# Feed-forward input of a ViT tower: normalising on ScalarE and weighing on GpSimd in place of VectorE

## Chip, cores and metric

One NeuronCore of a Trainium2 chip runs the whole program. The metric is device microseconds of that core for one execution. Before the change it is 2668.47 us (median of 3 runs, 2664.71 to 2668.48).

## The reference, cut to what matters

Four images become 12544 tokens of width 192, which go through a token attention, a linear attention, a routed feed-forward layer, a second attention and a quantised feed-forward layer. The change lies in the last of these:

```python
def rmsnorm(x, g):
    return x * jax.lax.rsqrt(jnp.mean(x * x, axis=-1, keepdims=True) + EPS_NORM) * g
def activation_quant(x):
    scale = 127.0 / jnp.maximum(jnp.max(jnp.abs(x), axis=-1, keepdims=True), EPS_Q)
    return jnp.clip(jnp.round(x * scale), -128, 127) / scale
...
h = bitlinear(x, w_in, g_in)
up, gate = jnp.split(h, 2, axis=-1)
y = jax.nn.silu(gate) * up
return bitlinear(y, w_out, g_out)
...
h = h + _L1_ffn_ref(_layernorm(h, axis=-1), L1_ffn_w_in, L1_ffn_g_in, L1_ffn_w_out, L1_ffn_g_out)
```

The layer norm and the RMS norm behind it come down to one factor per token: the input of the first product is (h - mean) * fac * g_in, which is then scaled by its largest absolute value and rounded to whole numbers.

## The kernel before

The last phase, `attention_and_ffn_phase`, handles the second attention and then the feed-forward layer. Tokens stand in `h` as 112 partitions by 112 tiles of 192 values. Four tiles are a group (448 tokens), and there are 28 groups (`NC`), seven to an image. The attention loop runs over s = 0 to 27; the feed-forward loop over g = 0 to 27 follows, and its first part (group 0 and the first input) is woven into the end of the attention loop. In the groups g = 1 to 7 (called the late groups here) the attention's output of the last image is added too (`map_late` on TensorE, `add_half` on VectorE); from g = 8 on there is only the feed-forward work.

There is no scheduler: each engine has a block of code, issues its instructions in the order written there, and waits at semaphores that are written out by hand. An instruction that waits holds up all that stands behind it on its engine.

One group g goes round as follows.

- VectorE, `quant_in(g+1)` (L2479 on): from the largest absolute value of each token to the scale `sx` and the output scale `dx`, with two small products by `fac` on the way (L2482, L2486), then four rounding instructions (L2488) and one that writes the whole numbers (L2493).
- VectorE, `weigh_in(g+2)` (L2464): four instructions write (h - mean) * gin to the single buffer `xg`; `largest_in(g+2)` (L2470) reduces it.
- TensorE, `into(g, q)` (L2048): two products per tile q = 0 to 3, the gate half and the up half. ScalarE, `silu(g, q)` (L2230); VectorE, `gated(g, q)` (L2501) multiplies the halves to `y`.
- GpSimd, `weigh(g, 0)` and `weigh(g, 1)` (L1872): y * gout for tiles 0, 1 and for tiles 2, 3, as `yg5`. VectorE, `largest_y(g, 0)` and `(g, 1)` (L2510) reduce these pairs. ScalarE, `squares(g, q)` (L2240) sums the squares; VectorE, `mean_square(g)` (L2506), and GpSimd, `root_of(g)` (L1877), make of them a factor per token.
- VectorE, `quant_y(g)` (L2525 to L2537): small instructions, the last of which (L2532) writes the scale `s2`, then the rounding of tiles 2 and 3. ScalarE, `scaled_y(g)` (L2247) rounds tiles 0 and 1 and `whole_y` (L2253) writes the whole numbers.
- TensorE, `transpose_y(g)` (L2060), ScalarE `take_y(g)` (L2259), TensorE `outof(g, pair)` (L2081), VectorE `result(g, pair)` (L2547), and SyncE stores the group.

ScalarE's order in a group is `scaled_y(g-1)`, `whole_y`, `take_y(g-1)`, squares 0, silu 2, squares 1, silu 3, squares 2, squares 3, `take_x(g+1)`, silu 0 and 1 of group g+1. The instruction of VectorE's `weigh_in` and GpSimd's loop are these:

```python
ins_ = nc.vector.scalar_tensor_tensor(xg[:, q, :], h[:, t, :], mean[:, t:t + 1], gin[:], ALU.subtract, ALU.mult)
...
for g in range(NC):
    weigh(g, 0)
    weigh(g, 1)
    root_of(g)
```

`fac` is made by GpSimd in one instruction for the first 64 tiles (`factor5(0, ...)`, L1864) while the attention loop ends, and in two more behind groups 8 and 9 for the rest.

Of the kernel before, what the change touches and what calls it, by code (L numbers as in the profile page):

```python
# [10 lines left out]
ACT = mybir.ActivationFunctionType  # L11
ALU = mybir.AluOpType
# [5 lines left out]
D = 192  # L18
KC = 96
T = 112  # L20
# [1630 lines left out]
def attention_and_ffn_phase(nc, ins, h, bns, mean, rstd, var, minus, eye, rows_out, out):  # L1651
# [9 lines left out]
    with ExitStack() as ctx:  # L1661
# [64 lines left out]
        fac = sb("fac5", [T, NT])  # L1726
        dif = rstd
        xg = sb("xg5", [T, TPC, D])
        xr = rows[:, TPC * HID:TPC * HID + TPC * D].rearrange("p (q d) -> p q d", q=TPC)
# [27 lines left out]
        def pga(g, q):  # L1757
# [10 lines left out]
                  "sg_out", "y_out", "yg_out", "ssq_out", "r2_in", "r2_out", "yq_out", "ytr_mm", "yT_out", "o_mm",  # L1768
                  "o_out", "stored", "dvec", "dvec2", "xg_out", "am_out", "fac_in", "fac_out", "scaled", "d2_out",
                  "xr_out", "yr_out", "s2_out", "ya_out")  # L1770
# [35 lines left out]
        def _(pool):  # L1806
# [59 lines left out]
            def weigh(g, pair):  # L1866

                for q in (2 * pair, 2 * pair + 1):
# [3 lines left out]
                    nc.gpsimd.tensor_tensor(yg5[:, q, :], y[:, q, :], gout[:], ALU.mult).then_inc(F["yg_out"], 1)  # L1872

            def root_of(g):

                pool.wait_ge(F["r2_in"], g + 1)
                nc.gpsimd.tensor_tensor(r2[:], ms2[:], mhalf5[:, 0:TPC], ALU.pow).then_inc(F["r2_out"], 1)  # L1877

            factor5(0, slice(0, HEAD))
            pool.wait_ge(F["gin_in"], 32)  # L1880
            for g in range(NC):
                weigh(g, 0)
                weigh(g, 1)
                root_of(g)
                if g in (AFTER, AFTER + 1):
                    half = HEAD + (g - AFTER) * (NT - HEAD) // 2
                    factor5(1 + g - AFTER, slice(half, half + (NT - HEAD) // 2))
# [260 lines left out]
        def _(act):  # L2148
# [77 lines left out]
            def silu(g, q):  # L2226
                act.wait_ge(F["in_mm"], g * TPC + q + 1)
                if 1 <= g * TPC + q <= TPC:
                    act.wait_ge(F["y_out"], g * TPC + q)
                nc.scalar.activation(sg[q % 2 if g else 0], pga(g, q)[0:T], ACT.Silu, scale=dx[g % 2][:, q:q + 1]).then_inc(  # L2230
                    F["sg_out"], 1)

            def squares(g, q):

                if g * TPC + q:
                    act.wait_ge(F["ssq_out"], g * TPC + q)
                if q == 0 and g:
                    act.wait_ge(F["r2_in"], g)
                act.wait_ge(F["y_out"], g * TPC + q + 1)
                nc.scalar.activation(junk5, y[:, q, :], ACT.Square, accum_out=ssq[:, q:q + 1]).then_inc(  # L2240
                    F["ssq_out"], 1)
# [14 lines left out]
            def take_y(g):  # L2256
                for half in range(2):
                    act.wait_ge(F["ytr_mm"], 2 * g + half + 1)
                    nc.scalar.copy(yT[:, 2 * half:2 * half + 2, :],  # L2259
                                   pyt[:, half, 0:2 * CH].rearrange("p (k c) -> p k c", k=2)).then_inc(F["yT_out"], 1)  # L2260

            take_x(0)
            silu(0, 0)
            silu(0, 1)
            for g in range(NC):
# [7 lines left out]
                squares(g, 1)  # L2273
                silu(g, 3)
                squares(g, 2)
                squares(g, 3)
# [10 lines left out]
        def _(dve):  # L2287
# [171 lines left out]

            def weigh_in(g):  # L2460

                for q in range(TPC):
                    t = g * TPC + q
                    ins_ = nc.vector.scalar_tensor_tensor(xg[:, q, :], h[:, t, :], mean[:, t:t + 1], gin[:],  # L2464
                                                          ALU.subtract, ALU.mult)
                ins_.then_inc(F["xg_out"], 1)

# [11 lines left out]
            def quant_in(g):  # L2479
                dve.wait_ge(F["fac_out"], 1 if (g + 1) * TPC <= HEAD else 3)  # L2480
                dve.wait_ge(F["am_out"], g + 1)
                scaling(nc.vector.tensor_tensor(am[:], am[:], fac[:, g * TPC:(g + 1) * TPC], ALU.mult))  # L2482
                scaling(nc.vector.tensor_scalar(am[:], am[:], 1e-5, 1.0 / 127, ALU.max, ALU.mult))
                nc.vector.tensor_scalar(dx[g % 2][:], am[:], wsc[0:T, 0:1], None, ALU.mult)
                scaling(nc.vector.reciprocal(sx[:], am[:]))
                scaling(nc.vector.tensor_tensor(sx[:], sx[:], fac[:, g * TPC:(g + 1) * TPC], ALU.mult))  # L2486
                for q in range(TPC):
# [69 lines left out]
            for s in range(-3, NC):  # L2557
# [30 lines left out]
                if s == NC - 2:  # L2588
                    dve.wait_ge(F["gin_in"], 32)
                    weigh_in(0)  # L2590
                    largest_in(0)
                if s == NC - 1:
                    quant_in(0)
                    weigh_in(1)
                    largest_in(1)
            gram_turned(B - 1)
# [7 lines left out]
            map_projected(B - 1)  # L2604
            add_half(NC - LATE + 1, 1, 0)
            quant_in(1)
            gated(0, 2)
            largest_y(0, 0)
            image_mapped(B - 1)
            weigh_in(2)  # L2610
            gated(0, 3)
            largest_in(2)
            mean_square(0)
            largest_y(0, 1)
            quant_y(0)
            for g in range(1, NC):
                late = NC - CPI + g - 1
                if g + 1 < NC:
                    quant_in(g + 1)
                if g + 2 < NC:  # L2620
                    weigh_in(g + 2)
                gated(g, 0)
                gated(g, 1)
                if g + 2 < NC:
                    largest_in(g + 2)
                gated(g, 2)
# [10 lines left out]
                if late < NC:  # L2637
                    add_half(late, 1, 0)
                result(g - 1, 1)
                quant_y(g)  # L2640
                if g == AFTER:
                    finish(1, slice(HEAD, NT))
            result(NC - 1, 0)
            result(NC - 1, 1)
# [110 lines left out]
```

## Time and profile before

| | |
|---|---|
| median of 3 runs | 2668.47 us |
| the profiled execution's own time | 2666.92 us |
| its span | 2665.1 us |
| granted TensorE clock, mean of the span | 0.912 of full speed |
| TensorE matmul busy, whole span | 84% |
| VectorE busy | 72% |
| ScalarE busy | 60% |
| GpSimd busy | 39% |

The span is one execution, seen by the hardware profiler. Busy shares are averages over phases with different limits, so the last phase has to be read by itself: the feed-forward loop lies between some 2234 us and the end. The timeline lists instructions in order of time, merged where the same instruction repeats; in square brackets is the idle time of the engine just before, and who ended it.

### The profile page before, as it was taken

What the parts mean: (1) busy time and instruction counts of PE and PEld (TensorE: products, weight loads), DVE (VectorE), ACT (ScalarE), POOL (GpSimd) and SP (SyncE); (2) the same over time, 40 slices, a digit from 0 to 9 for tenths busy, and PEclk for the clock granted to TensorE, in tenths of its full rate; (3) what the DMA queues carried; (4) which work ended last, traced back from release to release, by engine and by line L of the source; (5) the groups of instructions that cost most, each with busy time, mean ns of one, the idle gap of its engine ahead of it and who ended that gap; (6) DMA issues with size and microseconds to landing.
All of it is one profiled execution on the core that took longest, in us unless ns stands there. A gap on an engine that the chain in (4) does not pass through costs nothing. (4 is left out here: it accounts for less than half of the span.)

```text
span 2665.1 us, 45416 instructions
## 1 busy us (share of the span) xinstructions
PE 2250.9 (84%) x14046; PEld 1626.4 (61%) x14047; DVE 1924.3 (72%) x5417; ACT 1594.4 (60%) x2815; POOL 1040.1 (39%) x1101
## 2 busy tenths in 40 slices
PE   8999999999997899999982999991778887766655
PEld 4444444444443788888871999991667775544443
DVE  5777777777774688888872566664558778889896
ACT  2444444444443688888861676663778764667776
POOL 1100100100000167667673577676555533353433
PEclk9999999999998899999985999996779998777777
DMA  2000000000000333233235677777756720000000
GB/s 59 0 19 13 0 18 13 1 9 1 0 0 23 87 66 75 67 73 76 66 71 165 219 242 240 246 242 133 94 71 87 91 30 6 22 22 26 22 27 26
DMA packets 114522, 183.08 MB, mean 69 GB/s; under 512 B 14337, under 2 KB 84326, under 8 KB 114078
## 3 DMA queue, kind: packets, MB, share of 16 engines
q0 software_dynamic: 74816, 86.34, 17.3%
q1 hardware_dynamic: 39554, 94.84, 11.1%
q8 instruction: 80, 1.31, 0.2%
q14 instruction: 72, 0.59, 0.1%
HBM read 64.44 MB, written 64.39 MB: 48 GB/s over the span
## 5 line engine op out<-in xcount | busy, mean ns | idle before, releaser
L213 ACT ACTIVATE prob<-pscore 128x896 f32<-128x896 f32 x336 | 308.1, 917 | 423.5 <-PE pscore L295 423.5
L420 DVE TENSOR_REDUCE pmax<-ppre 112x1 f32<-112x512 f32 x656 | 424.3, 686 | 162.0 <-PE ppre L262 161.9
L309 PE MATMUL pout<-prob,xkey 128*64 128x448 f32 x1344 | 328.0, 567 | 0.4 <-ACT prob L213 0.4
L1578 POOL DMA_INDIRECT rows_out<-yb,home3b x252 | 244.5, 970 | 141.8 <-issue 59.3
L262 PE MATMUL ppre<-xh,yh 49*112 49x512 f32 x656 | 291.3, 446 | 7.8 <-DVE pmax L420 4.1
L195 POOL CAST yh<-ynext 113x448 fp32r<-113x448 f32 x28 | 17.2, 616 | 667.3 <-DVE pmax L420 639.2
L737 POOL DMA_INDIRECT rows_in<-xr,idx x224 | 235.1, 1050 | 76.3 <-issue 44.8
L262 PEld LDWEIGHTS ppre<-xh,yh 49*112 49x112 f32 x656 | 112.6, 172 | 239.5 <-issue 103.5
L295 PE MATMUL pscore<-yh,xh 49*128 49x448 f32 x700 | 241.2, 422 | 0.4 <-DVE yh L440 0.4
L1872 POOL TENSOR_TENSOR sums<-rows,gout 112x512 f32<-112x512 f32 x112 | 141.2, 1270 | 253.2 <-DVE rows L2501 253.2
L295 PE MATMUL pscore<-yh,xl 49*128 49x448 f32 x700 | 202.9, 364 | 0.0
L295 PE MATMUL pscore<-yl,xh 49*128 49x448 f32 x700 | 142.8, 364 | 0.0
L2060 PE MATMUL ptr<-eyeb,wT 112*128 112x112 bf16 x448 | 45.3, 292 | 114.1 <-ACT wT L2253 114.1
L1485 PE MATMUL pz<-xth3b,wd 128*128 128x448 f32 x504 | 140.7, 381 | 0.0
L1500 PE MATMUL py<-uph,zl 128*112 x504 | 131.8, 261 | 0.0
L1500 PE MATMUL py<-upl,zh 128*112 x504 | 131.6, 261 | 0.0
L1500 PE MATMUL py<-uph,zh 128*112 x504 | 131.5, 261 | 0.0
L309 PEld LDWEIGHTS pout<-prob,xkey 128*64 128x64 f32 x1344 | 66.6, 135 | 105.7 <-issue 85.3
L295 PEld LDWEIGHTS pscore<-yh,xl 49*128 49x128 f32 x700 | 127.9, 187 | 0.8
L1935 PE MATMUL pqk<-xh,wh 128*128 128x448 f32 x168 | 72.1, 429 | 56.4 <-ACT spent L2196 55.8
L2060 PEld LDWEIGHTS ptr<-eyeb,wT 112*128 112x128 bf16 x448 | 38.9, 141 | 126.8 <-ACT wT L2253 88.9
L1472 PE MATMUL ptr3b<-eye,xb 112*128 112x112 f32 x504 | 63.5, 271 | 61.9 <-DMA xb<-rows_in 42.8
(393 smaller groups left out, 6647.2 us busy)
## 6 DMA issues: line engine op xcount, KB each, us to landing
wd<-down SPq DMA_DIRECT2D x63, 512.0 KB
xb<-rows_in SPq DMA_DIRECT2D x63, 455.0 KB
sums<-rows_out POOLq DMA_DIRECT2D x56, 336.0 KB, 6.1
h<-brow POOLq DMA_DIRECT2D x28, 336.0 KB, 5.2
h<-gambet POOLq DMA_DIRECT2D x28, 336.0 KB, 4.9
out<-sums SPq DMA_DIRECT2D x28, 336.0 KB, 2.8
rows_in<-zero SPq DMA_DIRECT2D x15, 455.0 KB, 5.5
rows_out<-yb,home3b POOLq DMA_INDIRECT x252
```

The source lines that it names most:

```text
L213: nc.scalar.activation(prob[j % 3][:, :, :], pscore[j % 2][:, :, 0:CH], ACT.Exp).then_inc(exped, 1)
L262: pe.matmul(out[:, :], yh1[rows, q * T:(q + 1) * T], xh[b % 2][rows, block * 512:(block + 1) * 512], start=True, stop=True, tile_position= ...
L295: mm = pe.matmul(pscore[j % 2][:, i, 0:CH], x[b % 2][rows, keys], y[rows], start=(n == 0), stop=(n == 2), tile_position=(i * LO, 0))
L309: mm = pe.matmul(pout[i * LO:(i + 1) * LO, 0:CH], xkey[b % 2][:, 2 * j + i, :], prob[j % 3][:, i, :], start=(j == 0), stop=(i == 1 and j = ...
L420: nc.vector.reduce_max(pmax[:, q, 2 * block + half:2 * block + half + 1], bank(u, depth), AX.X).then_inc(pre_max, 1)
L737: nc.gpsimd.indirect_dma_start(rows_in, bass.IndirectOffsetOnAxis(ap=idx[r % G3][:, 2 * q + k:2 * q + k + 1], axis=0), xr[r % G3][:, q, :] ...
L1485: mm = pe.matmul(pz[m][:, 0:CH], wd[i][:, w, cols], x, start=(s_ == 0), stop=(s_ == 4))
L1500: mm = pe.matmul(py[i][:, q // 2, (q % 2) * D:(q % 2 + 1) * D], zz[i][m][:, cols], w[:, bass.ds(2 * e + m, 1), :], start=(m + n == 0), sto ...
L1578: nc.gpsimd.indirect_dma_start(rows_out, bass.IndirectOffsetOnAxis(ap=home[r][:, q:q + 1], axis=0), yb[r % 2][:, q, :], None).then_inc(ret ...
L1872: nc.gpsimd.tensor_tensor(yg5[:, q, :], y[:, q, :], gout[:], ALU.mult).then_inc(F["yg_out"], 1)
L1935: mm = pe.matmul(pqk[m % 2][:, 0:CH], w, x, start=(n == 0), stop=(n == 4))
L2060: mm = pe.transpose(pyt[:, half, k * CH + q * T:k * CH + (q + 1) * T], yq[:, q, (2 * half + k) * 128:(2 * half + k + 1) * 128], eyeb[0:T, ...
```

## The change

VectorE's `weigh_in` and the two small products by `fac` go. ScalarE gets `centre(g)`: four activations that write h * fac + off5 to `xg`, where off5 = -mean * fac is made by one VectorE instruction (`offset5`) for the first 64 tiles and one for the rest. GpSimd gets a new `weigh_in(g)`: one product over the whole group, in place, of `xg` with `gin`. VectorE's `largest_in(g+2)` moves from between the second and third `gated` of group g to just before `quant_y(g)`. `centre(g+2)` stands on ScalarE between silu 3 and squares 2 of group g, and GpSimd's `weigh_in(g+2)` between `weigh(g, 0)` and `weigh(g, 1)`.

```diff
@@ GpSimd
+            def weigh_in(g):
+                pool.wait_ge(F["xc_out"], g + 1)
+                nc.gpsimd.tensor_tensor(xg[:], xg[:], gin[:].unsqueeze(1).broadcast_to([T, TPC, D]),
+                                        ALU.mult).then_inc(F["xg_out"], 1)
             factor5(0, slice(0, HEAD))
             pool.wait_ge(F["gin_in"], 32)
+            weigh_in(0)
+            weigh_in(1)
             for g in range(NC):
                 weigh(g, 0)
+                if g + 2 < NC:
+                    weigh_in(g + 2)
                 weigh(g, 1)
                 root_of(g)
@@ ScalarE
+            def centre(g):
+                act.wait_ge(F["off_out"], 1 if (g + 1) * TPC <= HEAD else 2)
+                if g:
+                    act.wait_ge(F["xr_out"], g)
+                for q in range(TPC):
+                    t = g * TPC + q
+                    ac = nc.scalar.activation(xg[:, q, :], h[:, t, :], ACT.Identity, bias=off5[:, t:t + 1],
+                                              scale=fac[:, t:t + 1])
+                ac.then_inc(F["xc_out"], 1)
...
+            centre(0)
+            centre(1)
             take_x(0)
...
                 silu(g, 3)
+                if g + 2 < NC:
+                    centre(g + 2)
                 squares(g, 2)
                 squares(g, 3)
@@ VectorE
-            def weigh_in(g):
-                for q in range(TPC):
-                    t = g * TPC + q
-                    ins_ = nc.vector.scalar_tensor_tensor(xg[:, q, :], h[:, t, :], mean[:, t:t + 1], gin[:],
-                                                          ALU.subtract, ALU.mult)
-                ins_.then_inc(F["xg_out"], 1)
+            def offset5(n, cols):
+                dve.wait_ge(F["fac_out"], 1 + 2 * n)
+                nc.vector.scalar_tensor_tensor(off5[:, cols], mean[:, cols], -1.0, fac[:, cols], ALU.mult,
+                                               ALU.mult).then_inc(F["off_out"], 1)
             def quant_in(g):
-                dve.wait_ge(F["fac_out"], 1 if (g + 1) * TPC <= HEAD else 3)
                 dve.wait_ge(F["am_out"], g + 1)
-                scaling(nc.vector.tensor_tensor(am[:], am[:], fac[:, g * TPC:(g + 1) * TPC], ALU.mult))
                 scaling(nc.vector.tensor_scalar(am[:], am[:], 1e-5, 1.0 / 127, ALU.max, ALU.mult))
...
-                scaling(nc.vector.tensor_tensor(sx[:], sx[:], fac[:, g * TPC:(g + 1) * TPC], ALU.mult))
...
                 if s == NC - 2:
-                    dve.wait_ge(F["gin_in"], 32)
-                    weigh_in(0)
+                    offset5(0, slice(0, HEAD))
+                if s == NC - 1:
                     largest_in(0)
-                if s == NC - 1:
                     quant_in(0)
-                    weigh_in(1)
-                    largest_in(1)
...
             for g in range(1, NC):
...
-                if g + 2 < NC:
-                    weigh_in(g + 2)
                 gated(g, 0)
                 gated(g, 1)
-                if g + 2 < NC:
-                    largest_in(g + 2)
                 gated(g, 2)
...
                 result(g - 1, 1)
+                if g + 2 < NC:
+                    largest_in(g + 2)
                 quant_y(g)
...
+                if g == AFTER + 2:
+                    offset5(1, slice(HEAD, NT))
```

GpSimd's instructions of one group in the later part of the feed-forward loop, before (the product with `gout` is L1872, the root L1877):

```order
L1872 TENSOR_TENSOR sums<-rows,gout 112x512 x4
L1877 TENSOR_TENSOR r_5<-ms_5,mhalf 112x4
```

and with the change (the product with `gout` is L1873 there, the new one L1878, the root L1884):

```order
L1873 TENSOR_TENSOR sums<-rows,gout 112x512 x2
L1878 TENSOR_TENSOR xg<-xg,gin 112x768
L1873 TENSOR_TENSOR sums<-rows,gout 112x512 x2
L1884 TENSOR_TENSOR r_5<-ms_5,mhalf 112x4
```

The second pair of products with `gout` now stands behind the product for the input two groups on.

ScalarE in the same place with the change, from `scaled_y` to the copy of the next group's input (`sg_0` and `wqp` are the two buffers of silu, `spent` takes the squares, `maps` the transposed y, `xT` the transposed input):

```order
L2269 ACTIVATE xn<-sums,s_5 112x512 x2
L2275 ACTIVATE wT<-xn 112x1024 x2
L2281 COPY maps<-ptr 128x896 x2
L2262 ACTIVATE spent,ssq<-rows 112x512
L2241 ACTIVATE sg_0<-pqk_0,dx_0 112x512
L2262 ACTIVATE spent,ssq<-rows 112x512
L2241 ACTIVATE wqp<-pqk_1,dx_0 112x512
L2251 ACTIVATE xg<-h,minus,fac 112x192 x4
L2262 ACTIVATE spent,ssq<-rows 112x512 x2
L2235 COPY xT<-po 96x896
```

Before, the same row stands without L2251: the two last squares follow silu 3 at once.

VectorE in the same place with the change, from the last `gated` to the scale `s2` (L2553):

```order
L2522 SCALAR_TENSOR_TENSOR rows<-pg_1,dx_1,wqp 112x512
L2568 SCALAR_TENSOR_TENSOR sums<-po,d_5,h 112x192 x2
L2527 TENSOR_SCALAR ms_5<-ssq 112x4
L2531 TENSOR_REDUCE am_5<-sums 112x2
L2568 SCALAR_TENSOR_TENSOR sums<-po,d_5,h 112x192 x2
L2494 TENSOR_REDUCE am<-xg 112x4
L2546 COPY s_5<-r_5 112x4
L2547 TENSOR_TENSOR am_5<-am_5,r_5 112x4
L2550 TENSOR_SCALAR am_5<-am_5 112x4
L2551 RECIPROCAL s_5<-am_5 112x4
L2552 TENSOR_SCALAR d_5<-am_5,wsc 112x4
L2553 TENSOR_TENSOR s_5<-s_5,r_5 112x4
```

`largest_in` (L2494) now stands between the second `result` and the small instructions that end in `s2`.

## Rows read from the trace of the kernel before

**Rows 1.** The page, part 1: busy time, share of the span and instructions.

```profile
PE 2250.9 (84%) x14046; PEld 1626.4 (61%) x14047; DVE 1924.3 (72%) x5417; ACT 1594.4 (60%) x2815; POOL 1040.1 (39%) x1101
```

**Rows 2.** Stretches: length, then busy us of each engine; late groups, then groups 8 to 25.

```profile
2233.71:2354.67 120.96, 87.05 (x509) 64.86 (x507) 102.88 (x281) 77.27 (x135) 42.34 (x35) 0.77 0.06 18
2354.67:2621.16 266.49, 169.80 (x1005) 116.19 (x1006) 239.00 (x622) 197.45 (x341) 117.17 (x92) 0.74 0.09 24
```

**Rows 3.** Timeline, VectorE in one group: start, us, engine, line, instruction, [idle before].

```profile
2459.63 0.16 DVE L2532 TENSOR_TENSOR s<-s,r 112x4 f32<-112x4 f32 x1
...
2463.08 1.40 DVE L2464 SCALAR_TENSOR_TENSOR xg<-h,mean,gin 112x192 f32<-112x192 f32 x4
...
2467.44 0.75 DVE L2501 SCALAR_TENSOR_TENSOR rows<-pg,dx,sg 112x512 f32<-112x512 f32 x1 [0.78 <-PE pg L2048]
...
2470.82 0.59 DVE L2506 TENSOR_SCALAR ms<-ssq 112x4 f32<-112x4 f32 x1 [0.20 <-ACT spent L2240]
...
2474.16 0.15 DVE L2532 TENSOR_TENSOR s<-s,r 112x4 f32<-112x4 f32 x1
```

**Rows 4.** Timeline of the same group: the way from one s2 to the next.

```profile
2459.82 1.33 ACT L2247 ACTIVATE xn<-sums,s 112x512 f32<-112x512 f32 x2 [0.49 <-DVE s L2532]
...
2468.47 0.62 ACT L2240 ACTIVATE spent<-rows 112x512 f32<-112x512 f32 x1
...
2470.12 1.27 POOL L1872 TENSOR_TENSOR sums<-rows,gout 112x512 f32<-112x512 f32 x1 [0.51 <-DVE rows L2501]
...
2471.42 1.22 DVE L2510 TENSOR_REDUCE am<-sums 112x2 f32<-112x1024 f32 x1
...
2472.56 0.73 DVE L2547 SCALAR_TENSOR_TENSOR sums<-po,d,h 112x192 f32<-112x192 f32 x2
...
2473.21 0.16 DVE L2525 COPY s<-r 112x4 f32<-112x4 f32 x1
```

**Rows 5.** Groups by line: shapes, count, busy us, mean ns of one, idle before.

```profile
L2156 ACT ACTIVATE sums<-h,minus,rstd 112x192 f32<-112x192 f32 x112 | 51.7, 541 | 0.0
L1872 POOL TENSOR_TENSOR sums<-rows,gout 112x512 f32<-112x512 f32 x112 | 141.2, 1270 | 253.2 <-DVE rows L2501 253.2
L188 POOL TENSOR_TENSOR xl<-x,xh 113x1664 fp32r<-113x1664 f32 x3 | 11.3, 3752 | 0.2
L2470 DVE TENSOR_REDUCE am<-xg 112x4 f32<-112x768 f32 x28 | 26.4, 944 | 0.1
L2482 DVE TENSOR_TENSOR am<-am,fac 112x4 f32<-112x4 f32 x28 | 4.4, 156 | 0.0
```

**Rows 6.** Timeline of a late group.

```profile
2303.26 0.16 DVE L2532 TENSOR_TENSOR s<-s,r 112x4 f32<-112x4 f32 x1
...
2313.00 0.62 ACT L2240 ACTIVATE spent<-rows 112x512 f32<-112x512 f32 x1
...
2317.87 0.55 DVE L2346 TENSOR_TENSOR h<-h,po 112x384 f32<-112x384 f32 x1
...
2318.86 0.73 DVE L2547 SCALAR_TENSOR_TENSOR sums<-po,d,h 112x192 f32<-112x192 f32 x2
```

**Rows 7.** Timeline of the entry into the feed-forward loop.

```profile
2192.18 10.55 POOL L1864 TENSOR_TENSOR fac<-var,mhalf 112x64 f32<-112x64 f32 x1 [2.93 <-DVE var L2456]
...
2200.60 0.61 DVE L2331 TENSOR_TENSOR xl<-ptr,xh 128x448 fp32r<-128x448 f32 x1
...
2206.92 0.15 DVE L2482 TENSOR_TENSOR am<-am,fac 112x4 f32<-112x4 f32 x1
...
2208.13 0.21 ACT L2220 COPY maps<-pg 64x64 f32<-64x64 f32 x1
...
2208.90 0.56 DVE L2493 TENSOR_SCALAR gambet<-rows 112x768 bf16<-112x768 f32 x1
...
2227.15 0.69 ACT L2230 ACTIVATE sg<-pqk,dx 112x512 f32<-112x512 f32 x1 [3.05 <-PE pqk L2048]
...
2232.76 0.16 DVE L2525 COPY s<-r 112x4 f32<-112x4 f32 x1
```

More of the change, by code:

```diff
@@ L1727, in attention_and_ffn_phase @@
         dif = rstd
+        off5 = minus
         xg = sb("xg5", [T, TPC, D])
@@ L1768, in attention_and_ffn_phase @@
                   "sg_out", "y_out", "yg_out", "ssq_out", "r2_in", "r2_out", "yq_out", "ytr_mm", "yT_out", "o_mm",
-                  "o_out", "stored", "dvec", "dvec2", "xg_out", "am_out", "fac_in", "fac_out", "scaled", "d2_out",
+                  "o_out", "stored", "dvec", "dvec2", "xg_out", "xc_out", "off_out", "am_out", "fac_in", "fac_out", "scaled", "d2_out",
                   "xr_out", "yr_out", "s2_out", "ya_out")
@@ L2605, in _ @@
             add_half(NC - LATE + 1, 1, 0)
+            largest_in(1)
             quant_in(1)
@@ L2609, in _ @@
             image_mapped(B - 1)
-            weigh_in(2)
             gated(0, 3)
-            largest_in(2)
             mean_square(0)
             largest_y(0, 1)
+            largest_in(2)
             quant_y(0)
```

## The prediction

> **What bounds the kernel now.** The page's busy times come first: TensorE 84%, VectorE 72%, ScalarE 60%, GpSimd 39% of the span [rows 1]. These mix phases, and the change touches only the feed-forward loop, so the stretches come next. They are cut at the instruction that writes `s2`, one of which stands in each group. From group 8 to group 25 eighteen groups take 266.49 us, 14.80 us each, in which VectorE is busy for 239.00 (90%), ScalarE for 197.45 (74%, 10.97 a group) and GpSimd for 117.17 (44%); the seven late groups before them take 120.96 us, 17.28 each [rows 2]. The timeline of one group shows why VectorE sets the pace: it runs its list nearly without a gap, 0.78 us before the third `gated` and 0.20 before `mean_square` being what there is [rows 3]. ScalarE and GpSimd idle in between: GpSimd stood idle for 253.2 us before its products, waiting for `gated` [rows 5].
>
> So there is a list of 14.8 us on VectorE, and beside it a way from `s2` of one group to `s2` of the next that runs over other engines. That way has slack now. The question is whether the change, which shortens the list, lengthens the way beyond it.
>
> **What goes from VectorE.** `weigh_in` takes 1.40 us for its four instructions [rows 3], and each of the two small products about 0.16 [rows 5]: 1.72 us a group. `largest_in` (0.94) stays, at another place. If VectorE's list still set the pace, a group would take 14.80 - 1.72 = 13.08 us.
>
> **What ScalarE and GpSimd get.** `centre` is the same form as the activations with scale and offset of L2156, which read the same `h`: 112 of them busy ScalarE for 51.7 us, so four take 1.85 us [rows 5]. GpSimd's new product has 768 elements per partition. The rows have products of 512 elements (1.270 us) and of 1664 (3.752) [rows 5]: 2.482 us for 1152 more elements, so 256 more cost 0.55, and the product 1.82 us. Its bounds: no less than the 1.27 of the smaller one; and for the upper end I look at what the two engines do to each other. `mean_square` took 0.59 us, where a small instruction takes 0.16, and ended at 2471.41, just as GpSimd's product that began at 2470.12 ended (2471.39) [rows 3, 4]: some VectorE instructions are held until GpSimd's is over. If GpSimd were held in the same manner by the longest such instruction, the 0.56 us of L2493 [rows 7], its product would take 2.38.
>
> **The way from s2 to s2 with the change.** In the new order GpSimd does `weigh(g, 0)`, then waits for `centre(g+2)`, then multiplies, and only then turns to `weigh(g, 1)`. VectorE's `largest_y(g, 1)` waits for that last pair, and `quant_y`, which writes `s2`, is behind it. `centre(g+2)` itself stands on ScalarE behind silu 3 of group g, and that is behind `scaled_y(g-1)`, which waits for the `s2` before. So the parts close into a ring, group by group:
>
> - from `s2` (2459.63) over scaling, transposing and copying y, squares 0, silu 2, squares 1 and silu 3 to where the third square starts (2468.47): 8.84 us [rows 3, 4]. The work on TensorE within it is unchanged;
> - `centre`: 1.85; the hand-over to GpSimd 0.1 (an estimate: `s2` ends at 2459.79 and ScalarE starts at 2459.82, so it is no more) [rows 3, 4];
> - GpSimd: its new product 1.82, then the held-up pair, 2 x 1.27 = 2.54 [rows 5];
> - to `largest_y` 0.03 (2471.39 to 2471.42), which takes 1.14 until `result` starts at 2472.56, and that 0.65 until 2473.21 [rows 4];
> - `largest_in`, which now stands here: 0.94 [rows 5];
> - the small instructions to `s2`: 0.95 (2473.21 to 2474.16) [rows 3, 4].
>
> The sum is 18.86 us, against a list on VectorE of 13.1: the ring sets the pace. Before, the same way ran through VectorE's third and fourth `gated`, and GpSimd's last pair was over at 2471.39, just in time [rows 4]. ScalarE, with 10.97 + 1.85 = 12.8 us a group [rows 2], would not bind. The root on GpSimd, behind the pair, has the 2.73 us of the reductions and `result` to hide under. The stored result is never late, and no DMA is issued by GpSimd here.
>
> Groups 8 to 25: (18.86 - 14.80) x 18 = 73.0 us longer.
>
> Late groups: the first leg was 9.74 (2303.26 to 2313.00) [rows 6], in part because TensorE began behind VectorE's `gated`, which now comes 1.4 us earlier. I take the middle of 8.84 and 9.74, 9.3. The rest of the ring is 10.02, and one `add_half` with its statistics adds 0.99 (2317.87 to 2318.86) [rows 6]: 20.3 against 17.28, for seven groups 21.1 us.
>
> **Entry.** `offset5` waits for GpSimd's first `fac`, which ends at 2202.73; `low` behind it began at 2200.60 and comes 2.4 us later [rows 7]. TensorE is then still at products of the attention, so I let only 0.3 of this pass on (bounds 0 and 2.4). `centre(0)` starts when ScalarE is through with the attention, at 2208.34 [rows 7]; 1.85, 0.1, 1.82 and `largest_in` 0.94 follow, then the rest of `quant_in`, which took 2.54 from L2482 (2206.92) to the end of L2493 (2209.46) [rows 7] and loses 0.4 with the two products and their gaps. The first input is written at 2215.2 instead of 2209.46: 5.8, with the 0.3 some 6.1 us late. In group 0 the ring closes for the first time: silu 3, which ended at 2227.84, ends at 2233.9, and centre, hand-over, product, pair, `largest_y` and `largest_in` bring `quant_y(0)` to 2242.4 instead of 2232.76 [rows 7]. The entry costs 9.6 us.
>
> Groups 26 and 27 have no `centre`; I leave them as they are. The sum is 73.0 + 21.1 + 9.6 = 103.7 us on the profiled execution's own 2666.92: **2771 us**. The median of the runs is 1.5 us above that execution, which is small beside the bounds.
>
> **The rivals.**
>
> *The list on VectorE still sets the pace, and the change is a gain.* VectorE is the busiest engine of the stretch [rows 2], and 1.72 us a group leave it. With 25 groups of 13.08 us and 6 us for the first input the time would be 2667 - 43 + 6 = 2630 us. This decides where the ring is under 13.1 us, so 5.8 us of my ring would have to be hidden: centre, product and most of the pair. Nothing in the order hides them. 4%.
>
> [...]
>
> *The pair on GpSimd isn't what VectorE waits for last.* Then the ring goes over the two last squares (some 1.5 us with their readings) and `mean_square` instead of GpSimd: 8.84 + 1.85 + 1.5 + 0.2 + 1.14 + 0.65 + 0.94 + 0.95 = 16.1, so 23 us for groups 8 to 25, 2 for the late ones and 7 for the entry: 2699 us. It needs GpSimd's product and pair, 4.36 us, to fit into 1.7. 3%.
>
> *GpSimd's product is stretched by VectorE.* At 2.38 us, 25 rings get 0.56 longer: 2785 us. Against it: in the ring VectorE has little to do while GpSimd runs. 13%, and inside the range.
>
> **How the numbers follow.** 79% for my ring, 13, 4 and 3 for the rivals, 1 for no change. The range: downwards the product at 1.27 (-14), the late first leg at 8.84 (-3) and an entry 4 less give 2750; upwards the product at 2.38 (+14) and a first leg of 9.74 in all groups (+16, should TensorE's granted clock, 0.74 on average here [rows 2], fall further as it waits more) give 2802. Some 0.2% (5 us) is what a measurement of this kernel can tell from no change. Faster 0.04, same 0.01, slower 0.95.
>
> **What would show it.** Right: `s2` to `s2` near 18.9 us from group 8 on and 20.3 before; four `centre` in 1.85 and GpSimd's product in 1.82; its second pair behind that product in every group, with VectorE waiting some 2 to 3 us for GpSimd before `largest_y`; VectorE's busy share of the stretch down from 90% to some 61% ((239.0 - 31) / 339.5). Wrong: a spacing under 14.8, or `largest_y` that starts without a wait; a spacing near 16 would speak for the second rival, and a product over 2.2 us for the third.

## The result and the profile after

The changed kernel takes 2775.46 us (median of 4 runs, 2774.3 to 2776.58) against 2667.72 us for the kernel before, measured beside it (4 runs, 2664.71 to 2668.48). The ratio is 1.0406, with a 95% interval of 1.0388 to 1.0424: 108 us slower, where 2771 us were forecast.

The page, part 1, of the changed kernel, to be read beside [rows 1]:

```profile
PE 2279.1 (82%) x14046; PEld 1641.4 (59%) x14047; DVE 1880.8 (68%) x5251; ACT 1643.3 (59%) x2927; POOL 1083.5 (39%) x1129
```

VectorE lost 43.5 us of work (1924.3 to 1880.8), ScalarE and GpSimd gained 48.9 and 43.4. So the change did what it says, and the time went up all the same. The stretches, cut at `s2` as in [rows 2], show where (length, then busy us of TensorE, its weight load, VectorE, ScalarE and GpSimd, the granted clock, DMA):

```profile
2252.99:2391.90 138.91, 80.60 (x504) 61.39 (x504) 94.42 (x239) 88.66 (x161) 54.06 (x42) 0.76 0.06 17
2391.90:2729.52 337.62, 194.27 (x1008) 124.60 (x1008) 209.01 (x516) 230.15 (x414) 147.00 (x110) 0.61 0.07 19
```

A group takes 337.62 / 18 = 18.76 us from group 8 on, where it took 14.80, and a late group 19.84 where it took 17.28. VectorE is now busy for 209.01 of 337.62 us (62%, before 90%), ScalarE for 68%, TensorE for 58%: no engine's list sets the pace. What does is seen in the timeline of one group, which answers to [rows 3, 4]:

```profile
2504.28 0.16 DVE L2553 TENSOR_TENSOR s<-s,r 112x4 f32<-112x4 f32 x1
...
2504.48 1.33 ACT L2269 ACTIVATE xn<-sums,s 112x512 f32<-112x512 f32 x2 [2.40 <-DVE s L2553]
...
2513.36 1.85 ACT L2251 ACTIVATE xg<-h,minus,fac 112x192 f32<-112x192 f32 x4
...
2515.29 1.81 POOL L1878 TENSOR_TENSOR xg<-xg,gin 112x768 f32<-112x768 f32 x1 [4.57 <-ACT xg L2251]
...
2517.06 2.48 POOL L1873 TENSOR_TENSOR sums<-rows,gout 112x512 f32<-112x512 f32 x2
...
2519.57 1.22 DVE L2531 TENSOR_REDUCE am<-sums 112x2 f32<-112x1024 f32 x1 [2.45 <-POOL sums L1873]
...
2520.71 0.73 DVE L2568 SCALAR_TENSOR_TENSOR sums<-po,d,h 112x192 f32<-112x192 f32 x2
...
2521.36 0.94 DVE L2494 TENSOR_REDUCE am<-xg 112x4 f32<-112x768 f32 x1
...
2522.22 0.16 DVE L2546 COPY s<-r 112x4 f32<-112x4 f32 x1
...
2523.16 0.16 DVE L2553 TENSOR_TENSOR s<-s,r 112x4 f32<-112x4 f32 x1
```

It reads from one bracket to the next. GpSimd stands idle for 4.57 us and is released by ScalarE's `centre`; its product and then its pair follow without a gap; VectorE stands idle for 2.45 us and is released by that pair; ScalarE stands idle for 2.40 us and is released by `s2`. Each engine waits for another in turn, and the round closes in 2523.16 - 2504.28 = 18.88 us. (The rows show where the round waits; the steps between `s2` and `centre`, on ScalarE and TensorE, are the first leg of the prediction.)

The span grew from 2665.1 to 2772.6 us. By stages, in the two profiled executions:

| stage | before, us | after, us | longer by | forecast |
|---|---|---|---|---|
| start to the end of GpSimd's first `fac` | 2202.73 | 2210.48 | 7.75 | 0 |
| entry: from there to `s2` of group 0 | 30.98 | 42.51 | 11.53 | 9.6 |
| seven late groups | 120.96 | 138.91 | 17.95 | 21.1 |
| groups 8 to 25 | 266.49 | 337.62 | 71.13 | 73.0 |
| from there to the end | 43.94 | 43.08 | -0.86 | 0 |

The first stage holds nothing of the change. Its end lies between 2199.29 and 2210.48 in the ten kernels of this study, which have the same instructions up to the last steps of it; so 7.75 us is within the spread of these kernels. Matched instruction by instruction, the two traces lie within 1 us of each other up to some 800 us and then drift apart in steps up to the end of the stage. Whether that belongs to this kernel or to the execution that was profiled isn't shown (its four runs lie within 2.3 us), and the cause stays open.

### The profile page after: what moved, and what is told of

Same layout as the page of the kernel before. It is cut to its first block and busy times, and to the rows that moved or that the text cites. A ratio compares the mean times of both kernels' runs of the same rounds, so it can differ in the third digit from the quotient of the medians.

```text
span 2772.6 us, 45390 instructions
## 1 busy us (share of the span) xinstructions
PE 2279.1 (82%) x14046; PEld 1641.4 (59%) x14047; DVE 1880.8 (68%) x5251; ACT 1643.3 (59%) x2927; POOL 1083.5 (39%) x1129
## 5 line engine op out<-in xcount | busy, mean ns | idle before, releaser
L1873 POOL TENSOR_TENSOR sums<-rows,gout 112x512 f32<-112x512 f32 x112 | 139.5, 1266 | 186.8 <-DVE rows L2522 186.8
L2059 PE MATMUL pqk<-winq,xT 96*112 96x512 bf16 x224 | 106.1, 571 | 17.9 <-ACT xT L2235 17.9
```

The costliest lines, as they stand in the source:

```text
L2059: mm = pe.matmul(dst[0:T], xT[:, c, q * T:(q + 1) * T], winq[:, c, o:o + HID], start=(c == 0), stop=(c == 1))
```

## The experiments

Each ratio is against runs of the kernel before on the same chip, whose medians are 2663.63 us for kernels 1 to 4 and 2666.32 for kernels 5 to 8; the first row is that of the result above. The terms of a kernel come from its own profiled execution: the entry, the mean spacing of `s2` in the late groups, and in groups 8 to 25 (called the steady spacing).

| kernel | median us | ratio (95%) | entry | late | steady |
|---|---|---|---|---|---|
| before | 2667.72 | | 30.98 | 17.28 | 14.80 |
| after | 2775.46 | 1.0406 (1.0388 to 1.0424) | 42.51 | 19.84 | 18.76 |
| 1 product twice | 2816.76 | 1.0565 (1.0526 to 1.0605) | 54.98 | 21.52 | 20.53 |
| 2 no product | 2701.1 | 1.0122 (1.0089 to 1.0156) | 46.60 | 17.34 | 15.92 |
| 3 product behind the pair | 2716.68 | 1.0188 (1.0157 to 1.0219) | 41.42 | 17.26 | 17.06 |
| 4 and the reduction behind `s2` | 2693.11 | 1.0096 (1.0065 to 1.0128) | 49.37 | 16.20 | 16.09 |
| 5 and `centre` behind the squares | 2699.15 | 1.0111 (1.0085 to 1.0137) | 46.79 | 16.45 | 16.11 |
| 6 after, with the old entry | 2753.92 | 1.0327 (1.0304 to 1.035) | 31.10 | 20.00 | 18.75 |
| 7 as 5, with the old entry | 2684.22 | 1.0064 (1.0045 to 1.0082) | 31.07 | 16.48 | 16.04 |
| 8 as 7, product on VectorE | 2672.17 | 1.0026 (1.0013 to 1.0038) | 31.12 | 16.96 | 15.15 |

### 1. The product twice

```diff
                 pool.wait_ge(F["xc_out"], g + 1)
+                nc.gpsimd.tensor_tensor(xs5, xg[:], gin[:].unsqueeze(1).broadcast_to([T, TPC, D]), ALU.mult)
                 nc.gpsimd.tensor_tensor(xg[:], xg[:], gin[:].unsqueeze(1).broadcast_to([T, TPC, D]),
```

> The changed kernel with GpSimd's product of the input done twice, the first time into a spare buffer. Ring theory (GpSimd's product and the held-up pair lie on the way from s2 to s2): each of the 25 rings gets one product longer, 1.81 us, so s2 to s2 goes from 18.76 to 20.6 us from group 8 on; with the product of the first input and of group 2's input, 25 x 1.81 + 2 x 1.81 = 49 us, some 2824 us. Rival (GpSimd has 7 us of idle time in a group and VectorE doesn't wait for it last): s2 to s2 stays at 18.8, and the time within 5 us of 2775. Rival (the loss is TensorE's lower granted clock): no more than a few us.

Measured: 2816.76 us, somewhat under the 2824 of the ring and far from the 2775 of its rival. The total says little by itself: the profiled execution's entry grew by 12.47 us, where I had counted two products, and the stage ahead of it was 11.19 us shorter. The groups decide. Groups by line, groups 8 to 25 (busy us and mean ns, then idle time of the engine just before, and what ended it):

```profile
L1879 POOL TENSOR_TENSOR sums<-xg,gin 112x768 f32<-112x768 f32 x18 | 32.6, 1810 | 77.4 <-ACT xg L2253 75.4 <-DVE rows L2524 2.0
...
L2533 DVE TENSOR_REDUCE am<-sums 112x2 f32<-112x1024 f32 x36 | 43.7, 1215 | 76.4 <-POOL sums L1874 76.4
```

The added product takes 1.81 us on GpSimd, which is idle more than half of the time, and the steady spacing grows by 20.53 - 18.76 = 1.77: nearly its whole length is on the ring. VectorE's idle time before `largest_y` is 76.4 us in 18 groups; in the changed kernel, in the same stretch, it is 44.6, so the 32.6 us of GpSimd's added products came out, but for 0.8, as VectorE's wait. It answers the last rival too: TensorE's granted clock in the stretch is 0.61 in the changed kernel and 0.74 in this one, and the first leg, from `s2` to the start of `centre`, is 8.95 and 8.96 us in the mean of the 18 groups. So the lower clock isn't what makes the steady group long.

### 2. No product

The activations signal VectorE's reduction directly, and GpSimd's `weigh_in` is left out.

```diff
-            weigh_in(0)
-            weigh_in(1)
             for g in range(NC):
                 weigh(g, 0)
-                if g + 2 < NC:
-                    weigh_in(g + 2)
                 weigh(g, 1)
@@ ScalarE
-                ac.then_inc(F["xc_out"], 1)
+                ac.then_inc(F["xg_out"], 1)
```

> The changed kernel without GpSimd's product: ScalarE's centring hands its result straight on, so the multiplication by the input weights is left out. Ring theory: one product and one hand-over less, 1.9 us a ring, but the pair is no longer held up by centring either, so the ring goes over the two last squares and mean_square: 8.84 + 1.85 + 1.5 + 0.2 + 1.14 + 0.65 + 0.94 + 0.95 = 16.1 us at the least, 16.9 if the pair's wait were kept; 25 x (1.9 to 2.7) + 4 = 51 to 71 us less, 2704 to 2724 us. Rival (VectorE's shorter list of 13.1 us sets the pace once GpSimd is out of the way): 2640 us. Rival (ScalarE's work, 12.8 us a group, is the cause): no change, 2775.

Measured: 2701.1 us, a little under the range expected, steady spacing 15.92. Groups by line, the same stretch:

```profile
L2527 DVE TENSOR_REDUCE am<-sums 112x2 f32<-112x1024 f32 x36 | 43.6, 1211 | 0.7 <-POOL sums L1873 0.7
...
L2523 DVE TENSOR_SCALAR ms<-ssq 112x4 f32<-112x4 f32 x18 | 3.5, 193 | 19.7 <-ACT spent L2258 19.7
```

The wait for GpSimd is gone (0.7 us) and 19.7 us of waiting for ScalarE's squares are left. That is the prediction's second rival (16.1), the ring over the last squares: with the product out of the way it is the next thing that is late. The group is 2.84 us shorter, more than the product's 1.81, since GpSimd's second pair no longer waits for `centre` either.

### 3. The product behind the pair and the root

```diff
                 weigh(g, 0)
-                if g + 2 < NC:
-                    weigh_in(g + 2)
                 weigh(g, 1)
                 root_of(g)
+                if g + 2 < NC:
+                    weigh_in(g + 2)
```

> The changed kernel with GpSimd's product moved behind the second pair and the root of its group; nothing else is touched. Ring theory: the pair is no longer held up, but the reduction of the input still stands before the scale s2 and waits for the product, which now stands behind the root: 8.84 + centring 1.85 + two squares 1.5 + mean_square 0.2 + root 1.0 + product 1.81 + reduction 0.94 + small instructions 0.95 + hand-overs 0.2 = 17.3 us from group 8 on and about as much in the late groups: 18 x 1.5 + 7 x 2.5 + 2 = 46 us less, 2730 us. Rival (only the place of the product on GpSimd was at fault): VectorE's list sets the pace at 13 to 15 us a group, 2650 to 2690 us.

Measured: 2716.68 us, less than expected, with a steady spacing of 17.06 where I had 17.3. All the work is there, and 1.70 us a group from group 8 on are gone by order alone. The timeline of one group shows the new wait:

```profile
2514.98 1.80 POOL L1878 TENSOR_TENSOR xg<-xg,gin 112x768 f32<-112x768 f32 x1
...
2516.82 0.95 DVE L2494 TENSOR_REDUCE am<-xg 112x4 f32<-112x768 f32 x1 [1.13 <-POOL xg L1878]
```

VectorE no longer waits before `largest_y` but before `largest_in`, which stands ahead of `s2`: a scale of this group is held up by a reduction that is wanted two groups on. Over the 18 groups that wait is 20.2 us, 1.12 a group.

### 4. The reduction behind `quant_y`

```diff
                 result(g - 1, 1)
+                quant_y(g)
                 if g + 2 < NC:
                     largest_in(g + 2)
-                quant_y(g)
```

> As the kernel with GpSimd's product last, and in addition VectorE's reduction of the input moves behind the instructions that write s2. Ring theory: product and reduction leave the way to s2; what stays is 8.84 + 1.85 + 1.5 + 0.2 + largest_y 1.14 + result 0.65 + 0.95 = 15.1 us, plus what ScalarE comes late to s2, up to 0.6; 15.1 to 15.7 us from group 8 on, 16 to 17 in the late ones, and the entry of 11 us stays: some 2690 us (2680 to 2700). Rival (VectorE's list): 13.1 to 14 us a group, 2640 to 2660 us. Rival (GpSimd's product is not the point): 2775.

Measured: 2693.11 us, steady spacing 16.09. I expected 15.1 to 15.7. The timeline of one group shows what took the rest:

```profile
2506.08 1.81 POOL L1878 TENSOR_TENSOR xg<-xg,gin 112x768 f32<-112x768 f32 x1
...
2506.72 1.21 DVE L2546 COPY s<-r 112x4 f32<-112x4 f32 x1
...
2507.95 0.16 DVE L2547 TENSOR_TENSOR am<-am,r 112x4 f32<-112x4 f32 x1
```

A copy of four values, which takes 0.16 us in the changed kernel, takes 1.21 here, and ends (2507.93) when GpSimd's product ends (2507.89). It is the first of the small instructions of `quant_y`. In each of the 18 groups it ends 0.02 to 0.03 us after the product, and its mean is 1.197 us: some 1.04 us a group are given back. 16.09 less 1.04 is 15.05, an estimate, since not every group need lose the whole of it.

### 5. `centre` behind the squares and the copy

```diff
                 silu(g, 3)
-                if g + 2 < NC:
-                    centre(g + 2)
                 squares(g, 2)
                 squares(g, 3)
                 if g + 1 < NC:
                     take_x(g + 1)
+                    if g + 2 < NC:
+                        centre(g + 2)
```

> As the kernel with GpSimd's product last and the reduction behind s2, and in addition ScalarE's centring moves from between silu 3 and squares 2 to behind the copy of the next group's input, ahead of its silu 0. Ring theory: the 1.85 us of centring leave the way to s2, which then runs over the fourth gated product and GpSimd's pair as in the kernel before (about 13.9 us by its rows); VectorE's copy at the head of the small instructions was held for 1.05 us by GpSimd's product in the kernel of the step before, and stays so; ScalarE comes up to 1 us later to s2. 15 to 16 us from group 8 on, about 16 in the late groups, some 2680 us. Rival (GpSimd's hold on VectorE grows instead): 16.1 us and 2693 us as without this step.

Measured: 2699.15 us where I expected 2680; the steady spacing is 16.11, so the rival, a longer hold by GpSimd, came true. `centre` is no longer on the chain of work that the profile follows back through this stretch, and GpSimd's product with it starts later and falls on another instruction of `quant_y`:

```profile
2510.52 1.82 POOL L1878 TENSOR_TENSOR xg<-xg,gin 112x768 f32<-112x768 f32 x1 [0.92 <-ACT xg L2251]
...
2510.70 1.67 DVE L2550 TENSOR_SCALAR am<-am 112x4 f32<-112x4 f32 x1
...
2512.40 0.18 DVE L2551 RECIPROCAL s<-am 112x4 f32<-112x4 f32 x1
```

L2550 takes 1.583 us in the mean of the 18 groups, 0.170 in the changed kernel; in 17 of them it ends 0.02 to 0.03 us after the product, and in the one where it starts behind the product it takes 0.17. Mainly by that, VectorE's busy time in the stretch comes to 238.37 us, where it was 209.01 for the same work in the changed kernel: a busy share can be time held.

### 6. The changed kernel with the old entry

Groups 0 to 2 get their input from VectorE's old `weigh_in` and the two products by `fac`, in their old places; from group 3 on all is as in the changed kernel.

```diff
+            def weigh_old(g):
...
             def quant_in(g):
                 dve.wait_ge(F["am_out"], g + 1)
+                if g < 3:
+                    dve.wait_ge(F["fac_out"], 1)
+                    scaling(nc.vector.tensor_tensor(am[:], am[:], fac[:, g * TPC:(g + 1) * TPC], ALU.mult))
...
                 if s == NC - 2:
-                    offset5(0, slice(0, HEAD))
-                if s == NC - 1:
+                    dve.wait_ge(F["gin_in"], 32)
+                    weigh_old(0)
                     largest_in(0)
```

> The changed kernel with the first three inputs made as before, on VectorE and with the two small products. Theory (TensorE idles at the start of the feed-forward work until the first input is there, and its granted clock falls to the lower level for what follows): the stretch from the end of the first fac to the first s2 goes back from 42.5 (46 to 55 in other kernels of this study) to 31 us, with TensorE's granted clock near full until about the last third of it; rings unchanged at 19.84 and 18.76 us: 2755 to 2766 us. Rival (the entry's loss is only GpSimd's and ScalarE's own time in the chain of the first input, 6 us): 2768 to 2770 us.

Measured: 2753.92 us, just under the expected 2755. The entry is back at 31.10 us (before 30.98), 11.4 us shorter than in the changed kernel, and the steady spacing stays at 18.75. So the two parts add up, and the entry's share comes with the placement of the first three groups. How much of the 11.4 us is the longer chain of the first input and how much TensorE's clock, this run doesn't separate. (The 46 to 55 us of the expectation leave out kernel 3, whose entry took 41.42.) The medians of the two kernels differ by 21.5 us, their profiled executions by 19.9; 9.46 of that lie ahead of the entry (2210.48 against 2201.02), in the first stage of the table above.

### 7. Kernel 5 with the old entry

The edit is that of 6 on kernel 5; L2550 of kernel 5 is L2559 here.

> Both: old entry, centring behind the copy of the next input, GpSimd's product last, reduction behind s2. Entry 31, late groups 16.0 to 16.2, from group 8 on 15 to 16, tail 43: 2655 to 2680 us, the same as the kernel before within 0.5%. VectorE's list is 1.7 us shorter than before and buys nothing, because the way from s2 to s2 is about 14 us even without the input on it. Rival (VectorE's list set the pace before and does again): 13.1 us a group, 2635 us.

Measured: 2684.22 us, ratio 1.0064 (1.0045 to 1.0082), just above the expected range. The entry is 31.07 and the steady spacing, 16.04, that of kernel 5; the same instruction takes 1.583 us in the mean again.

### 8. The product on VectorE

The edit is against kernel 7.

```diff
                 root_of(g)
-                if g and g + 2 < NC:
-                    weigh_in(g + 2)
@@ VectorE
             def largest_in(g):
+                if g > 2:
+                    dve.wait_ge(F["xc_out"], g - 2)
+                    nc.vector.tensor_tensor(xg[:], xg[:], gin[:].unsqueeze(1).broadcast_to([T, TPC, D]),
+                                            ALU.mult).then_inc(F["xg_out"], 1)
                 dve.wait_ge(F["xg_out"], g + 1)
```

> As the one with the old entry and everything moved, but the product with the input weights is done by VectorE, one instruction over the group just before the reduction (a product of that form takes 0.95 us in the trace of before); ScalarE still centres. VectorE's list is 14.80 - 1.72 + 0.95 = 14.0 us, GpSimd has no product of the input, so its hold on the small instructions ahead of s2 (1.05 us) goes. If that hold is what keeps the way long: 14.2 to 15.0 us from group 8 on, 5 to 18 us less than with GpSimd's product, some 2645 to 2660 us. Rival (ScalarE's lateness at s2 is what keeps it long): no difference to the kernel with GpSimd's product.

Measured: 2672.17 us (12 runs) against 2666.32 (17 runs): 1.0026 (1.0013 to 1.0038), so still a little slower than before, and slower than I expected. The stretch of groups 8 to 25, and two groups by line of it:

```profile
2353.10:2625.83 272.73, 176.90 (x1005) 118.56 (x1006) 226.63 (x534) 225.19 (x413) 116.91 (x92) 0.72 0.08 24
```

```profile
L2533 DVE SCALAR_TENSOR_TENSOR rows<-pg,dx,sg 112x512 f32<-112x512 f32 x36 | 26.9, 748 | 32.6 <-PE pg L2055 32.6
...
L2497 DVE TENSOR_TENSOR xg<-xg,gin 112x768 f32<-112x768 f32 x18 | 17.1, 951 | 0.0
```

The product costs VectorE 0.95 us, not 1.81, and holds nobody. VectorE's list is 226.63 / 18 = 12.6 us, yet the spacing is 15.15: it stands idle for 32.6 / 18 = 1.8 us a group before the third `gated`, until TensorE brings its products. With the list shortened by some 0.7 us (239.00 to 226.63 in 18 groups), the loop is held by a way over TensorE, ScalarE and VectorE that is about as long as the old spacing (14.83 us in a group of that trace). `centre` on ScalarE is part of that way in some groups. Which part of it could be shortened was not tried. None of the kernels beat the one before.

## Why the prediction was right

**The ring, right.** By its terms, forecast and then measured in the group shown: first leg 8.84 and 9.08 (8.84 in the next group); `centre` and hand-over 1.95 and 1.93; product 1.82 and 1.77 to the pair's start; the pair with its hand-over 2.57 and 2.51; `largest_y` 1.14 and 1.14; `result` 0.65 and 0.65; `largest_in` 0.94 and 0.86; the small instructions 0.95 and 0.94. The sum is 18.86 against 18.88, and 18.76 over 18 groups. That it is so close is in part luck: the 8.84 was read from one group, and in the 18 groups of the kernel before the same leg lies between 8.47 and 10.38 us (mean 9.23; changed kernel 8.95). The durations held over the whole loop (groups by line, 2200 us to the end):

```profile
L2531 DVE TENSOR_REDUCE am<-sums 112x2 f32<-112x1024 f32 x56 | 68.0, 1214 | 64.3 <-POOL sums L1873 64.2
...
L2251 ACT ACTIVATE xg<-h,minus,fac 112x192 f32<-112x192 f32 x112 | 51.8, 535 | 4.6 <-DVE rows L2509 4.6
L1878 POOL TENSOR_TENSOR xg<-xg,gin 112x768 f32<-112x768 f32 x28 | 50.7, 1811 | 129.6 <-ACT xg L2251 129.6
```

The product's 1.82 was worked out from two other sizes and measures 1.811; the third rival (2.38) is out. Experiment 1 shows that it is on the ring with nearly its whole length, and experiment 3 that 1.70 us a group of the loss come from its place on GpSimd's queue and not from its work; in its new place VectorE still waits 1.12 us for it.

**The first rival, VectorE's list, wrong as forecast, and with it the prediction's account of the kernel before.** A busy share of 90% was true and said nothing of the gain: the list got shorter by (239.00 - 209.01) / 18 = 1.67 us a group, and the group longer by 3.96. The prediction held that VectorE's list set the pace before and that the way from `s2` to `s2` had slack. The trace of the kernel before speaks against it. Its groups 8 to 25, by line, and then the chain that the profile follows back through one group (start, us, what):

```profile
L2501 DVE SCALAR_TENSOR_TENSOR rows<-pg,dx,sg 112x512 f32<-112x512 f32 x36 | 26.9, 748 | 17.3 <-PE pg L2048 15.0 <-ACT sg L2230 1.2 <-POOL sums L1872 1.1
```

```profile
2445.11 0.17 DVE s L2532
...
2445.30 1.33 ACT xn L2247 x2
2446.64 1.90 ACT wT L2253 x2
...
2448.58 1.68 PE ptr L2060 x16
...
2453.60 0.70 ACT wqp L2230
...
2454.71 0.75 DVE rows L2501
...
2459.63 0.17 DVE s L2532
```

VectorE waits 17.3 / 18 = 0.96 us a group before the third `gated`, mostly for TensorE, and `weigh_in` stands ahead of that wait. In the group shown the chain goes from `s2` over ScalarE and TensorE to VectorE's last `gated` and the next `s2`, without `weigh_in`; over the 18 groups only 0.23 of the 1.40 us of `weigh_in` are on it. So the way set the pace in most groups already. That work taken from VectorE ahead of the wait had little to gain, even with a ring no longer than before, follows from it but was not tried by itself. The forecast didn't rest on that account, since it set the new ring against the measured spacing of 14.80.

The Trainium skill (Perfetto Trace Analysis, section "Optimizing Scalar/DVE Operations") says that with VectorE saturated it may make sense to give work to ScalarE or even GpSimd, and that between GpSimd and VectorE it might not help, since they share a read port. VectorE's 90% met the condition, and the kernel got 4% slower. The longer way cost that, and not the port: on the ring the product's 1.81 us and the small instructions' 0.94 are the lengths forecast without any hold. Experiments 4, 5 and 8 took the ring apart and still did not reach the shorter list.

**The late groups, 0.46 us a group too high.** One of them, timeline:

```profile
2312.83 0.16 DVE L2553 TENSOR_TENSOR s<-s,r 112x4 f32<-112x4 f32 x1
...
2321.98 1.85 ACT L2251 ACTIVATE xg<-h,minus,fac 112x192 f32<-112x192 f32 x4
...
2332.78 0.16 DVE L2553 TENSOR_TENSOR s<-s,r 112x4 f32<-112x4 f32 x1
```

The first leg is 9.15 (I took 9.3) and the rest 10.80 (11.01); other groups are shorter yet. The term came to 17.95 instead of 21.1.

**The entry, 1.9 us too low.** The first input is written 12.67 us after `fac` where it took 6.73, so 5.9 us late (forecast 6.1). From there to `s2` of group 0 it takes 29.84 us where it took 24.25: 5.6 longer, where the prediction's terms left 3.5. TensorE's timeline shows what they had not counted:

```profile
2211.57 0.49 PE L1958 MATMUL po<-wimg,xTB 65*112 65x192 f32 x2
...
2216.33 0.33 PE L1979 MATMUL pqk<-eye,maps 128*128 128x128 f32 x1 [1.03 <-ACT maps L2231]
2223.30 0.95 PE L2046 MATMUL ptr<-eyeb,gambet 112*96 112x112 bf16 x8 [6.64 <-DVE gambet L2514]
...
2224.78 0.85 PE L1958 MATMUL po<-wimg,xTB 65*112 65x192 f32 x2
```

TensorE stands idle for 6.64 us, waiting for the first input, and afterwards the same pair of products takes 0.85 us instead of 0.49. The stretch from the first input to `s2`, in the kernel before, in the changed one, and in kernel 2:

```profile
2209.50:2233.71 24.21, 17.99 (x97) 12.34 (x98) 20.79 (x60) 7.66 (x15) 6.08 (x5) 0.89 0.00 1
```

```profile
2223.15:2252.99 29.84, 22.71 (x100) 15.32 (x100) 17.95 (x49) 11.36 (x24) 9.54 (x7) 0.73 0.00 1
```

```profile
2213.56:2249.46 35.90, 31.93 (x98) 21.32 (x99) 17.60 (x49) 10.67 (x23) 6.07 (x5) 0.50 0.00 0
```

About a hundred matmuls each time; the granted clock is 0.89, 0.73 and 0.50 of full speed (0.50 is the lower of its two levels), and TensorE's busy time 18.0, 22.7 and 31.9 us. Kernel 2 has less on the way (no product) and its first input is sooner after `fac` than in the changed kernel, and still its entry is 4.1 us longer. How the 1.9 us divide between the clock and the way isn't separated by these runs. That they are no more is luck too: kernels 3 and 4 wait for the first input as long as the changed kernel, and their entries took 41.42 us at a clock of 0.74 and 49.37 at 0.50 (the last section has all of them).

**The tail, right** (forecast 0, measured -0.86).

**The sum.** The terms of the change, with the tail, come to 11.53 + 17.95 + 71.13 - 0.86 = 99.75 us, against 103.7. The remaining 7.75 us of the span's difference lie ahead of the change. So the total came out nearer (2775 against 2771) than the terms deserve: they were 4 us too high, and a stage outside them was 8 longer.

## What to carry to other kernels

Before work is taken off the busiest engine, follow the way from one instruction of a group to the same instruction of the next over all engines, in the order of their queues; if that ring with the moved work is longer than a group takes now, the change loses by the difference. A busy engine that waits for another in every group, as VectorE did here for some 1 us, is a sign that a ring sets the pace already. Look at what the moved instruction is put in front of: the largest single step back here, 58.8 us of the 103.3 between the changed kernel and kernel 8 (7.6 of them in the first stage), was moving the product behind the pair that was waited for, without changing any work. At the entry of a loop, where the ring is run through once without cover, every step of a longer way counts, and in each of the six kernels here whose TensorE had to wait there for 4.7 us or more its granted clock was lower afterwards.

## What the runs showed of the hardware

**GpSimd's products hold small VectorE instructions.** In kernels 4 and 5 a copy and a tensor-with-scalar instruction (L2550) on four values per partition went from 0.16 and 0.17 us to 1.21 and 1.67 and ended with GpSimd's product. A reduction was not: in kernel 4 one ran beside such a product, and both took their usual time.

```profile
2501.42 1.21 DVE L2531 TENSOR_REDUCE am<-sums 112x2 f32<-112x1024 f32 x1
...
2501.65 1.27 POOL L1873 TENSOR_TENSOR sums<-rows,gout 112x512 f32<-112x512 f32 x1 [1.27 <-DVE rows L2522]
```

The Trainium skill, SBUF — State Buffer, section "Who interferes with whom", says that VectorE and GpSimd share a pair of ports that is locked for a whole instruction, that `copy` and `tensor_scalar` can need it and `tensor_reduce` never does on this chip. The rows above agree with that. In the kernel before, the timeline shows a GpSimd instruction that does not hold:

```profile
2371.48 4.17 POOL L1864 TENSOR_TENSOR fac<-var,mhalf 112x24 f32<-112x24 f32 x1 [4.07 <-DVE var L2456]
...
2371.63 0.17 DVE L2483 TENSOR_SCALAR am<-am 112x4 f32<-112x4 f32 x1
...
2372.18 0.16 DVE L2486 TENSOR_TENSOR sx<-sx,fac 112x4 f32<-112x4 f32 x1
```

The instruction that makes `fac` raises one tensor to the power of another and runs for 4.17 us, and VectorE's small instructions, one with two inputs in SBUF among them, take their usual time beside it. So that both are a TENSOR_TENSOR on GpSimd is not enough to tell; the rows have to be looked at.

**TensorE's clock after a wait.** The wait of TensorE for the first input, the granted clock (1 is full speed) from that input to `s2` of group 0, the length of that stretch and TensorE's busy time in it:

| kernel | wait, us | clock | stretch, us | busy, us |
|---|---|---|---|---|
| before | 0.89 | 0.89 | 24.25 | 17.99 |
| 6, 7 and 8 | 0.89 | 0.84 | 24.37 | 19.2 to 19.3 |
| 2 | 4.70 | 0.50 | 35.90 | 31.93 |
| changed | 6.64 | 0.73 | 29.84 | 22.71 |
| 3 | 6.64 | 0.74 | 28.77 | 22.66 |
| 4 | 6.64 | 0.50 | 36.74 | 32.76 |
| 5 | 6.64 | 0.50 | 34.13 | 31.54 |
| 1 | 8.40 | 0.50 | 40.56 | 33.40 |

The same wait of 6.64 us was followed by two outcomes. In kernels 4 and 5 the clock stayed at its lower level through the whole stretch, though TensorE was busy for most of it; in the changed kernel and in kernel 3 it came back in between. Kernel 4 differs from kernel 3 in the place of one reduction on VectorE, which leaves its way to `s2` shorter, and its stretch is still 8.0 us longer. What decides how long the lower clock lasts, these runs don't show.
